# Edge rows joined in the first stage, and attention layers without ScalarE's bias passes

## What is computed

```python
# L0: three graph attention layers, 4 heads of 24
h = (x @ W).reshape(N, H, C)
e = leaky_relu(alpha_s[src] + alpha_d[dst], 0.2)
ex = exp(e - segment_max(e, dst)[dst])
out = segment_sum(h[src] * (ex / segment_sum(ex, dst)[dst])[:, :, None], dst) + b
x = relu(out)
# L1: segment_sum(x[src], dst) + (1+eps)*x, two-layer MLP, batch norm
# L2: attention of scaled products over the same edges, clipped to [-10, 10]
# L3: messages relu(x[src] + edge_attr @ We + be) summed by dst, MLP, batch norm
```

## Time and profile before

| | us |
|---|---|
| runs | 5854.73, 5863.40, 5868.62 |
| median | 5863.4 |
| profiled execution | 5863.81, of which the span 5862.1 |
| first stage, until the tables start | 1647.2 |
| tables | 1647 to about 1950 |
| three attention layers | about 1950 to 4025 |
| the rest | about 4025 to the end |

### The profile page before, as it was taken

The page is one execution under the profiler, slowest core; times in us unless marked ns, Lnnn a source line. Parts: engine busy times, 40 slices in busy tenths (PEclk is TensorE's granted clock), DMA queues, the critical chain, the costliest instruction groups (busy, mean ns, idle before and its releaser), DMA issues. The chain is left out here.

```text
span 5862.1 us, 68109 instructions
## 1 busy us (share of the span) xinstructions
PE 3511.6 (60%) x25247; PEld 2219.0 (38%) x25248; DVE 3123.5 (53%) x3383; ACT 2625.6 (45%) x4143; POOL 3883.7 (66%) x3309
## 2 busy tenths in 40 slices
PE   3211222221034699988999889997868781667764
PEld 2211111111034455555555555554433330455542
DVE  3644555554369555445555455555579992333323
ACT  1000000000023689888888789894059891222211
POOL 1888888888884577666776578773020787777772
PEclk7555555555566899999999999998989995677765
DMA  8222222222279699757997479875542332332222
GB/s 296 20 18 20 20 18 10 1 1 0 9 251 361 169 195 199 161 115 150 195 193 156 103 164 201 184 153 152 178 166 79 109 130 74 110 81 74 75 53 24
DMA packets 427191, 683.75 MB, mean 117 GB/s; under 512 B 177678, under 2 KB 272397, under 8 KB 422768
## 3 DMA queue, kind: packets, MB, share of 16 engines
q0 software_dynamic: 236096, 287.22, 31.9%
q1 hardware_dynamic: 172432, 350.48, 17.8%
q10 hardware_dynamic: 18336, 41.70, 2.1%
HBM read 540.73 MB, written 138.43 MB: 116 GB/s over the span
## 5 line engine op out<-in xcount | busy, mean ns | idle before, releaser
L330 POOL DMA_INDIRECT counts<-plcell_add,plcell_slot x806 | 1253.9, 1556 | 385.4 <-issue 223.2
L1704 POOL DMA_INDIRECT emxg<-xtab,emsrc x856 | 944.0, 1103 | 448.4 <-issue 257.8
L714 ACT ACT_TABLE_LOAD x1 | 1.3, 1283 | 1613.2 <-PE mtps L702 1613.2
L377 PE MATMUL plpsR<-plpiece,plbefore 128*128 128x500 bf16 (+1 forms) x81 | 47.1, 582 | 813.8 <-DVE plranked L507 800.6
L422 DVE TENSOR_REDUCE plnlow<-plsame 128x13 f32<-128x1664 bf16 x62 | 117.0, 1888 | 661.6 <-DMA counts<-plcell_add,plcell_slot 661.5
L1788 PE MATMUL dotbanks<-emmsg,emsame 128*128 128x96 f32 x1712 | 316.3, 344 | 237.4 <-DVE emsame L1968 230.1
L1176 ACT ACTIVATE ga1prob<-ga1psE,ga1src_fifth 128x512 f32<-128x512 f32 (+1 forms) x700 | 407.2, 680 | 81.8 <-PE ga1psE L1281 79.1
L1176 ACT ACTIVATE ga2prob<-ga2psE,ga2src_fifth 128x512 f32<-128x512 f32 (+1 forms) x700 | 407.5, 683 | 77.0 <-PE ga2psE L1281 74.1
L1176 ACT ACTIVATE ga0prob<-ga0psE,ga0src_fifth 128x512 f32<-128x512 f32 (+1 forms) x700 | 407.1, 678 | 77.7 <-PE ga0psE L1281 74.7
L1788 PEld LDWEIGHTS dotbanks<-emmsg,emsame 128*128 128x128 f32 x1712 | 287.2, 250 | 382.2 <-issue 379.5
L1281 PE MATMUL ga0psE<-ident,ga0logit 128*128 128x128 f32 x2500 | 394.5, 288 | 55.8 <-DMA ga0logit<-log_counts 32.7
(11 more groups left out here) (403 smaller groups left out, 8577.9 us busy)
## 6 DMA issues: line engine op xcount, KB each, us to landing
ga0logit<-log_counts POOLq DMA_DIRECT2D x88, 512.0 KB
ga1logit<-log_counts POOLq DMA_DIRECT2D x88, 512.0 KB
ga2logit<-log_counts POOLq DMA_DIRECT2D x88, 512.0 KB
counts<-plzeros SPq DMA_DIRECT2D x32, 1250.0 KB, 32.7
mthalf<-counts SPq DMA_DIRECT2D x50, 800.0 KB
log_counts<-mtlogs SPq DMA_DIRECT2D x25, 1600.0 KB
ginhalf<-counts SPq DMA_DIRECT2D x50, 800.0 KB
dotlogs<-log_counts ACTq DMA_DIRECT2D x25, 1600.0 KB
```

The costliest lines, as they stand in the source:

```text
L330: nc.gpsimd.indirect_dma_start(counts[w][:, :], bass.IndirectOffsetOnAxis(ap=cell_slot[:, g % 2, j:j + 1], axis=0), cell_add[:, g % 2, j:j ...
L377: nc.tensor.matmul(psR[:, f // RANK_BANK, 0:k * BINS], before[:], piece[:, n % 2, f:f + k, :].rearrange("p t b -> p (t b)"), start=True, s ...
L714: nc.scalar.activation(logs[:, n % OUTS, q, :], ps[:, u % 3, 0:BW], ACT.Ln, bias=tiny[:, 0:1], scale=math.e).then_inc(log_made, 1)
L1704: nc.gpsimd.indirect_dma_start(xg[:, h, t, :], None, xtab[:, :], bass.IndirectOffsetOnAxis(ap=src[:, g, t:t + 1], axis=0)).then_inc(gather ...
```

## The change

It has three parts.

1. In the first stage SP loads the edge features of a group from DRAM into `whole` (three buffers of [128, 13, 34]), ACT puts the two end nodes behind the 32 features, and SP stores the joined rows in DRAM (`edge_rows`). SP's waits on `added[1]` spread this over the stage, a group for every four adds, after the last clear of `sorted_edges`. `edge_scatter` then issues one load per group instead of four loads and two copies, with the slots loaded once. The stores of tile columns, needs and slots stand behind the loop, and the stage waits for all stores of rows.
2. In the attention layers DVE clamps all tiles, and adds the loaded `mask` to tiles 0 and 1 in a second instruction (`tensor_tensor` in place of `scalar_tensor_tensor`). ACT's `add_bias` is gone.
3. The small tails of the two tables are zeroed ahead of the large parts, from one partition.

```diff
@@ begin, SP
                 for part, done in zip(counts, zeroed):
+                    sp.dma_start(part[NP * NP:NP * NP + P, :].rearrange("(p f) o -> p (f o)", p=1), zeros[0:1, 0:P]).then_inc(done, 16)
+                for part, done in zip(counts, zeroed):
                     v = part[0:NP * NP, :].rearrange("(p j f) o -> j p (f o)", p=P, f=ZF)
                     for j in range(ZEROS):
                         sp.dma_start(v[j], zeros[:]).then_inc(done, 16)
-                    sp.dma_start(part[NP * NP:NP * NP + P, :], zeros[:, 0:1]).then_inc(done, 16)
...
+                features = a["edge_attr_32"]
+                most = features[0:(P - 1) * ET, :].rearrange("(p t) k -> p t k", t=ET)
+                rest = features[(P - 1) * ET:E, :].rearrange("(p t) k -> p t k", p=1)
+
+                def load_whole(g):
+
+                    k = g % WHOLE_BUFS
+                    if g >= WHOLE_BUFS:
+                        sp.wait_ge(whole_stored[k], 16 * (g // WHOLE_BUFS))
+                    sp.dma_start(whole[0:P - 1, k, :, 0:ED], most[:, g * G:(g + 1) * G, :]).then_inc(whole_loaded[k], 16)
+                    n = min(G, EREST - g * G)
+                    if n > 0:
+                        sp.dma_start(whole[P - 1:P, k, 0:n, 0:ED], rest[:, g * G:g * G + n, :]).then_inc(whole_loaded[k], 16)
+
+                sp.wait_ge(whole_cleared, 1)
+                load_whole(0)
+                for g in range(NG):
+                    sp.wait_ge(added[1], 16 * (4 * SORTED_GROUPS + 2 * g + 1))
+                    if g + 1 < NG:
+                        load_whole(g + 1)
+                    sp.wait_ge(whole_made, g + 1)
+                    sp.dma_start(edges["rows"][:, g * G:(g + 1) * G, :], whole[:, g % WHOLE_BUFS, :, :]).then_inc(whole_stored[g % WHOLE_BUFS], 16)
...
-                sp.dma_start(edges["ends"][:, :, :], ends[:]).then_inc(stored, 16)
                 sp.dma_start(edges["slot"][:, :], block_i[:]).then_inc(stored, 16)
@@ begin, ACT
+                for g in range(NG):
+                    act.wait_ge(whole_loaded[k], sum(32 if n * G < EREST else 16 for n in uses))
+                    nc.scalar.activation(whole[:, k, :, ED:RW], ends[:, g * G:(g + 1) * G, :], ACT.Copy).then_inc(whole_made, 1)
@@ edge_scatter
-            pool.dma_start(slot[:, m, :], edges["slot"][:, g * G:(g + 1) * G]).then_inc(list_loaded[m], 16)
-            pool.dma_start(ends[:, m, :, :], edges["ends"][:, g * G:(g + 1) * G, :]).then_inc(list_loaded[m], 16)
-            pool.dma_start(rows[0:P - 1, :], most[:, g * G * ED:(g + 1) * G * ED]).then_inc(feat_loaded[k], 16)
-                pool.dma_start(rows[P - 1:P, 0:n * ED], rest[:, g * G * ED:(g * G + n) * ED]).then_inc(feat_loaded[k], 16)
+            pool.dma_start(stage[:, k, :, :], edges["rows"][:, g * G:(g + 1) * G, :]).then_inc(rows_loaded[k], 16)
...
-            nc.gpsimd.tensor_copy(stage[:, k, :, 0:ED], feat[:, k, :, :]).then_inc(staged, 1)
-            nc.gpsimd.tensor_copy(stage[:, k, :, ED:RW], ends[:, m, :, :]).then_inc(staged, 1)
@@ gat_attend
+                def clamp_kept(r, q):
+                    if r >= L_BUFS:
+                        dve.wait_ge(turned, run_end(r - L_BUFS))
+                    nc.vector.tensor_scalar(logit[:, r % L_BUFS, q, 0:width], src_row[:, h, first:first + width], dst_bias[:, j % 2, q, h:h + 1],
+                                            low_bias[:, j % 2, q, h:h + 1], ALU.add, ALU.max).then_inc(kept_clamped, 1)
                 def finish_logit(r, q):
-                    dve.wait_ge(act_biased, act_count[r] + kept_tiles(j).index(q) + 1)
-                    nc.vector.scalar_tensor_tensor(part, src_row[:, h, first:first + width], least[:, block_first[j] + q, h:h + 1], part, ALU.max, ALU.add).then_inc(logit_ready, 1)
+                    dve.wait_ge(kept_clamped, kept_count[r] + kept_tiles(j).index(q) + 1)
+                    dve.wait_ge(mask_loaded[k], 16 * (uses + 1))
+                    nc.vector.tensor_tensor(part, part, mask[:, k, 0:width], ALU.add).then_inc(logit_ready, 1)
-                def add_bias(r, q):
-                    nc.scalar.activation(logit[:, r % L_BUFS, q, 0:width], mask[:, k, 0:width], ACT.Identity, bias=dst_bias[:, j % 2, q, h:h + 1]).then_inc(act_biased, 1)
```

More of the change, by code:

```diff
@@ L120, in program @@
         halves_rows = [c[0:NP * NP, :].rearrange("(r c) o -> r (c o)", c=NP) for c in counts]
-        edges = {"slot": nc.dram_tensor("edge_slot", [P, ET], i32), "ends": nc.dram_tensor("edge_ends", [P, ET, 2], f32),
+        edges = {"slot": nc.dram_tensor("edge_slot", [P, ET], i32), "rows": nc.dram_tensor("edge_rows", [P, ET, RW], f32),
                  "column": nc.dram_tensor("tile_column", [T_CHUNKS * P, 1], i32), "need": nc.dram_tensor("tile_need", [T_CHUNKS * P, 1], i32),
@@ L205, in begin @@
         ends = sb("ends", [P, ET, 2])
+        whole = sb("whole", [P, WHOLE_BUFS, G, RW])
         earlier = sb("earlier", [P, P])
@@ L767, in source_rows, with edge_scatter @@
     return row_kept, len(chunks)
[L770 to L776, removed]
+def edge_scatter(nc, ctx, edges, tag, first, last):
+    STAGES = 3
     count = last - first
[L778 to L783, removed]
-    list_loaded = [sem(f"list_loaded{k}") for k in range(LISTS)]
-    feat_loaded = [sem(f"feat_loaded{k}") for k in range(STAGES)]
-    scattered = [sem(f"scattered{k}") for k in range(STAGES)]
-    def steps(pool):
-        nc.gpsimd.memset(feat[:], 0.0).then_inc(feat_cleared, 1)
-        pool.wait_ge(feat_cleared, 1)
-        flat = a["edge_attr_32"].rearrange("e k -> (e k)")
-        most = flat[0:(P - 1) * ET * ED].rearrange("(p f) -> p f", f=ET * ED)
-        rest = flat[(P - 1) * ET * ED:E * ED].rearrange("(p f) -> p f", p=1)
-        loads = lambda i: 32 if (first + i) * G < EREST else 16
+    slot = ctx.enter_context(nc.sbuf_tensor(tag + "slot", [P, max(count, 1) * G], i32))
+    stage = ctx.enter_context(nc.sbuf_tensor(tag + "stage", [P, STAGES, G, RW], f32))
+    slots_loaded = nc.alloc_semaphore(tag + "slots_loaded")
+    rows_loaded = [nc.alloc_semaphore(f"{tag}rows_loaded{k}") for k in range(STAGES)]
+    scattered = [nc.alloc_semaphore(f"{tag}scattered{k}") for k in range(STAGES)]
+    def steps(pool):
@@ L809, in steps @@
         load(0)
+        pool.wait_ge(slots_loaded, 16)
         for i in range(count):
-            k, m = i % STAGES, i % LISTS
+            k = i % STAGES
             if i + 1 < count:
                 load(i + 1)
-            pool.wait_ge(feat_loaded[k], sum(loads(n) for n in range(k, i + 1, STAGES)))
-            pool.wait_ge(list_loaded[m], 32 * (i // LISTS + 1))
-            if i >= STAGES:
-                pool.wait_ge(scattered[k], 16 * G * (i // STAGES))
-            nc.gpsimd.tensor_copy(stage[:, k, :, 0:ED], feat[:, k, :, :]).then_inc(staged, 1)
@@ L1096, in _ @@
                     for q in kept_tiles(0):
+                        clamp_kept(r, q)
+                    for q in kept_tiles(0):
                         finish_logit(r, q)
@@ L1106, in _ @@
                             clamp(r + AHEAD, q)
-                    for i in range(MOST + 1):
-                        if ahead is not None and i < len(kept_tiles(ahead)):
-                            finish_logit(r + AHEAD, kept_tiles(ahead)[i])
-                        if run == 2 and j and i == 1:
-                            output(j - 1)
+                        for q in kept_tiles(ahead):
+                            clamp_kept(r + AHEAD, q)
+                        for q in kept_tiles(ahead):
+                            finish_logit(r + AHEAD, q)
+                    if run == 2 and j:
+                        output(j - 1)
                     if run == RUNS - EARLY - 1 and j + 1 < BLOCKS:
```

68 lines of the change are left out of this document (34 added, 34 removed).

## The result

The changed kernel takes 6140.1 us (median of 5 runs, 6124.5 to 6143.9) against 5864.6 us for the kernel before (5 runs beside it): 1.046 times as long, interval 1.044 to 1.048. It is slower, as forecast, by 276 us where 486 were forecast. The profiled execution took 6132.1 us, its span is 6130.3 us (before: 5862.1).

What follows compares the result with a forecast made beforehand. It took POOL's 806 adds to bound the first stage, and ACT, PE and DMA to be loaded in the layers. 5863.8 + 646 (loads on one engine) - 160 (layers) = 6350 us; range 5950 to 7050.

Steps and rivals of the forecast that it cites:

- The price of a piece: First-stage load: each 128-byte piece costs 12 ns on one DMA engine, so 20.5 us a group with its store.
- The overlap with the adds: First stage: POOL's adds, keeping each DMA engine 22% busy until 1641, delay the loads by half of 154 us, 77.
- The share of 0.06: Sign in the profile after: DMA share near 0.06, about 10 GB/s, while POOL, DVE and PE idle some 650 us.
- The start: First stage: the loop of loads starts at 939 us, after SP's last clear at 938.8.
- Part 3, "nothing": Tails zeroed first: the first add may start up to 3 us earlier, with no gain in total time.
- The layers, -160: Attention layers without ACT's bias passes: 0.84 us gained per run, 64 runs a layer, 54 us a layer, 160 for three.
- DVE, not PE, ends a run: Attention layers, eight units without `sum_tops`: DVE's clamps and additions take 5.7 us, against 5.44 for PE and 6.54 before.
- The number of runs: Attention layers: 514 of 700 units in a layer lack `sum_tops`, 64 runs of 8.
- It is worth nothing by itself, only room: Tables and layers: POOL's one load instead of four and two copies frees POOL time but gains 0 us.
- the spread load: Rival, first stage: the load uses 16 engines, the stage keeps its end, total 5704 us; chance 0.13.

Runs made afterwards that it cites:

- e4: The changed kernel with each 127-partition load put down dense, one piece of 1664 bytes a partition, and joined by ACT: 6024.4 us.
- e3: The kernel before with only the tails of the two tables zeroed ahead of the large parts: 5840.0 us.
- e5: e1 with two PSUM buffers for the turned scores in the attention layers in place of three: 5827.1 us.
- e6: e1 with DVE's mask addition to kept tiles done on 64 columns only, so attention weights differ: 5605.5 us.
- e8: e1 with DVE's order for kept tiles clamp, addition, clamp, addition in place of both clamps, then both additions: 5667.6 us.
- e2: The kernel before with only the changed attention layers (DVE clamps and additions, no ACT bias pass), old edge loads on POOL: 5880.4 us.
- e7: e1 with the attention layers of the kernel before, so joined rows, split load and tails first: 5795.7 us.
- e1: The changed kernel with each 127-partition load issued as two, of 112 and 15 partitions: 5748.7 us.
- e11: e8 with a wait in front of nearly every clamp and addition on DVE: 5706.7 us.
- e10: e1 in its own order, but the second addition waits for the first and the next clamp for both: 5684.4 us.

## Why the prediction was right, and where it was off

Its sign and mechanism held: one DMA engine carried the load, as far as 14 GB/s, 9.4 ns a piece and e4's 0.93 of one engine show it, the stage grew, the layers gave a part back. The size was off in both terms.

**The price of a piece**, 12 ns, was too high; this is the mis-sized term. With the loads alone a group takes 16.8 us (1876.04 to 1892.84); less 0.7 us for the store, over 1664 pieces, that is 9.7 ns, and 9.4 in the stretch without a store. Over 62 groups the error is 62 x (20.5 - 16.8) = 229 us. The nearest rows from below were pieces of 96 bytes written as a load of all engines; the true value lies under both rows that I had interpolated between. One of the two prices taken from the earlier trace rows, 12.0 ns by share, is the time that a piece takes; here that is 13.0 ns, close to it, but the next piece begins after 9.4. The share gave the time of a piece and not the pace. Why the peak slice's rate gave 11.0 ns for smaller pieces, with the engines over 90% busy, is open.

**The overlap with the adds**, 77 us, was about right for the loads: a group took 17.8 us beside the adds and 16.8 after them, in 53 groups some 55 us. But the step took for granted that the adds wouldn't suffer; it named it only as what would prove it wrong. They did: 2.5 us in place of 1.87. Hidden here, it decides in e4. The share of 0.06 that it named as a sign was 0.09 between the stores.

**The start**, 939: 24 us too late. The first load went out at 915.4. 229 + 22 + 24 = 275 of the 277 us between 646 and 369. (22 is 77 less 55.) With 66 us less gained in the layers and 7 us elsewhere, 486 - 277 + 66 - 7 = 268 us, the difference of the profiled executions.

**Part 3, "nothing"**: 20 us (e3), within the 24 above. My reason looked at the adds' pace only, and not at where the small stores stood: the first table's was issued at 34.1 us, behind that table's 20 MB of zeros, and these two stores landed 41.6 us after their issue (median), beside the zeros of the second table.

**The layers, -160**: measured -94 in them. "DVE, not PE, ends a run", at 5.7 us, was wrong: PE and ACT handing three PSUM buffers to and fro end a regular run at 6.04 (e5 shows it, and e6, where DVE has less to do and the pace stays). The number of runs was wrong as well, and 3.27 us for four units was the quickest case of before: the next two in that timeline take 3.34 and 3.35 (products at 3020.40, 3023.74, 3027.09). 6.54 - 6.04 = 0.5 in place of 0.84, 64 times in each of three layers, is 96 us, but that this meets the measured 94 is luck: in the changed kernel 44 of the 168 runs of eight units go at the regular pace, and they gained 46 us. The rest lies in runs that something else ends; e8 frees another 83 us in them, 50 of these in the first two runs of the blocks.

**"It is worth nothing by itself, only room"**, said of the joined rows, fell with e2 and e7. POOL's waits for DVE had shown spare time on average; in the first runs of the blocks there was too little, by what e6 and e8 free there.

The runs by rivals: the spread load would have given 5704, and e1, where it is spread, takes 5749: the layers gave 71 us less than the term, the tails 20 us more than nothing. What stays open is at which of DVE's instructions a held scatter gets in; e11 shows that a pause at each isn't the rule, and the 3.81 us scatter that it gets in without one. The best kernel is e8: 5667.6 us, 3.3% below the kernel before and 7.7% below the changed one.

## What to carry to other kernels

Before a DMA is given 127 of 128 partitions, look for a transfer with an awkward number of them in the trace; if its share is that of one engine (0.07 for the 53 rows here), split it: a group went from 17.8 us to 7.7. Price the other transfers too: the adds beside it went from one per 1.87 us to one per 2.5. When a price comes from a DMA share, ask whether the pieces overlap (13.0 ns each here, one every 9.4). And where GpSimd issues DMAs beside VectorE, the order of VectorE's instructions and the waits between them are a resource: two long ones side by side cost a scatter 2.9 us here, with a clamp and a wait between them 0.9, and averages of waits don't show it.

## What the runs showed that was not expected

- One loaded DMA engine at a share of 0.24 to 0.28 slowed POOL's adds from one per 1.87 us to one per 2.5 (pieces of 128 bytes) and 3.0 (pieces of 1664 bytes); all sixteen at 0.47 left them at 104 in 200 us.
- SP is held by the DMA behind the long one (16.84 us), and not by the long one (0.24 us).
- Pieces of 128 bytes went at 14 GB/s, one every 9.4 ns, though each took 13.0 ns.
- A scatter on GpSimd took 0.95 us alone and up to 3.86 us beside VectorE's two-input additions and 3.76 us beside one-input pieces. Pauses of 0.13 us between the additions, in the same order, brought 64 us (e10); another order with pauses of 0.03 us brought 81 us (e8).
